# A decoder of six sublayers on one core: an attention's heads put in place by two transfers of 256 KB instead of four of 128 KB

## The chip, the cores and the metric

The kernel runs on one core of a Trainium2 chip. The metric is the device time of one execution in microseconds (us); the median of three runs before the change is 1601.11 us (1593.27 to 1602.95).

## What is computed

Sixteen sequences of 256 tokens and 256 channels go through two decoder layers of three sublayers each. After every sublayer its output is added to the stream and the sum is normalised (`_layernorm`):

```python
x = _layernorm(x + _L0_attn_ref(x, ...))            # 16 heads of 16, rotary, self
x = _layernorm(x + _L0_xattn_ref(x, ctx, ctx, ...)) # 8 heads, gated mLSTM-like mix
x = _layernorm(x + _L0_ffn_ref(x, ...))             # quantised, ternary weights
x = _layernorm(x + _L1_attn_ref(x, ...))            # 16 heads of 16, self
x = _layernorm(x + _L1_xattn_ref(x, ctx, ctx, ...)) # 16 heads of 16, cross
x = _layernorm(x + _L1_ffn_ref(x, ...))             # relu, 1024 wide
```

Three of the six are softmax attentions with 16 heads of 16 channels, and the change concerns these three only:

```python
attn = softmax(einsum('bhqd,bhkd->bhqk', q, k) * scale)
out = einsum('bhqk,bhkd->bhqd', attn, v)
return out.transpose(0, 2, 1, 3).reshape(B, N, C) @ w_proj + b_proj
```

## The kernel before

The 16 sequences are dealt to four lanes (L = 0 to 3), four sequences each, one after the other in a lane. Each lane has its own buffers and runs the same list of steps (`lane_steps`); the lanes are interleaved so that an engine that would wait for one lane works for another. Which lane an engine serves next is not decided while it runs: `TURNS` holds one string of digits per engine, and `engine_program` deals each lane's steps out in that order. So each of the five instruction queues (TensorE, ScalarE, VectorE, GpSimd, SyncE) is a fixed list worked off in order, with semaphore waits in it. `PLACES` says which PSUM banks a step of TensorE uses, and `FILL` how many extra products of a constant (line 688, tile `cst`, results never read) it does at the head of a step; both are fixed tables too.

One attention of one lane runs so. `max` (line 785 on TensorE, line 1198 on VectorE) finds the largest score of each row, `negmax` lays the negated maxima beside the queries (a small transfer, line 672), `exp` (line 804, then ScalarE's Exp on line 1025) makes the weights of two heads at a time in eight units, `pv` multiplies them with the values. The weights of a unit go to one of three places in turn: two halves of `PB` and, for units 2 and 5, the tile `YX`. The value products (line 822) come in four steps, `pv` 0 to 3, for four heads each. Each value has beside it a column of ones, so that a product of 32 rows holds the 16 channels of a head and 16 copies of the sum of its weights, row by row in turn. Two steps share a PSUM bank: ScalarE copies the results of `pv` 0 and 1 into `U[:, 0:2]`, and those of 2 and 3 into `U[:, 2:4]` (line 1029; each copy raises `u_ready`). The first of the two steps raises `pv_half`.

In `U` channels and sums alternate from row to row. The step `spread` on SyncE (line 668) sorts them with transfers inside SBUF: the channels to `OT`, the sums to `sums`, which are the two halves of `YX`, 64 rows per transfer, all four transfers behind one wait for the second copy. Then ScalarE's step `heads` waits for all of them (`spread`), takes the logarithm of the sums (line 1032) and the exponential of the negated logarithm (line 1034), GpSimd multiplies the channels with it (line 1357), and TensorE's step `proj` (line 712, `psum<-W_o,YX`) multiplies with the output weights. VectorE adds the stream (line 1204) and normalises. There are 3 × 16 = 48 such attentions. `W_o`'s rows are laid out to match the places of the heads when the weights are loaded.

SyncE's queue also carries everything else that moves: the queries and keys through DRAM (lines 653 and 656 out, line 662 back, `QK<-heads_dram`), the inputs (593, 597) and the outputs (675).

Of the kernel before, what the change touches and what calls it, by code (L numbers as in the profile page):

```python
# [16 lines left out]
P = 128  # L17
# [40 lines left out]
def lane_steps():  # L58

    out = []  # L60

    def add(name, occ=0, unit=0, ahead=0):
        out.append((name, occ, unit, ahead))

    def attention(a):
        if a:
            add("xT", a + 1)
            add("xb", a + 1)
            for name in ("qk", "stack"):
                for j in range(2 if a == 1 else 1):  # L70
                    add(name, a, j)
        if a == 1:
            add("v", 1)
        for u in range(PAIRS):
            add("max", a, u)
        add("negmax", a)
        for u in range(PAIRS):
            add("exp", a, u)
            if u in (2, 4, 6):
                add("pv", a, (u - 2) // 2)  # L80
        add("pv", a, 3)
        add("spread", a)
        add("heads", a)
        if a == 1:
            add("qk", 2, 1)
            add("stack", 2, 1)
            add("v", 2)
        if a == 2:
            add("loadx", 0, 0, 1)
        add("proj", a)  # L90
        add("norm", NORM_OF[a])

    attention(0)
    add("xT", 1)
    add("xb", 1)
    add("gates")
    add("vm")
    add("turn")
    add("decay", 0, 0)
    add("decay", 0, 1)  # L100
    add("mix", 0, 0)
    add("decay", 0, 2)
    add("mix", 0, 1)
    add("mixv", 0, 0)
    add("decay", 0, 3)
    add("mix", 0, 2)
    add("mix", 0, 3)
    add("mixv", 0, 1)
    add("mixnorm")
    add("mixvar")  # L110
    add("mixscale")
    add("mixout")
    add("norm", 1)
    add("quant")
    for t in range(TT):
        add("gate", 0, t)
        add("up", 0, t)
    for t in range(TT):
        add("hT", 0, t)
    add("down")  # L120
    add("norm", 2)
    attention(1)
    attention(2)
    add("loadc", 0, 0, 1)
    add("xT", 4)
    add("xb", 4)
    for u in range(4):
        add("up1", 0, u)
    add("xT", 0, 0, 1)
    for t in range(TT):  # L130
        add("rope", 0, t, 1)
    add("ctx", 0, 0, 1)
    add("v", 0, 0, 1)
    add("down1", 0, 0)
    for name in ("qk", "stack"):
        for j in range(2):
            add(name, 0, j, 1)
    add("down1", 0, 1)
    add("norm", 5)
    add("store")  # L140
    add("xb", 0, 0, 1)
    return out


def lane_program(lane):
# [7 lines left out]
    for at in range(-1, batches):  # L153
# [56 lines left out]
        "3312203100002112121112232223300003331311102313222303030011112223300220010331121012312203033300111102"  # L210
        "2323123002112333200112103302031133222233"),
    "sp": (
        "4330022110000111414022212303331224330000101114400122220001233331011122320122300331120000013322311111"
        "0232322230123333213233000011110122220001001323330111232200122303210000013332123111110232222323013333"
        "2133230000011110122220000123313301121032201202320000013333121212130111332222012333333123230000111101"
        "020202210013333012113022231223333210323213"),
}

PLACES = (
# [106 lines left out]
def decoder_kernel(nc, x, ctx, consts, w_qkv0, w_proj0, w_gates, b_gates, w_gate, w_up, w_down,  # L326
# [3 lines left out]
    with es:  # L330
# [50 lines left out]
        OT = XT_  # L381
        sums = [v[:, 0].rearrange("p (k t) -> p k t", k=KT) for v in YX]

        VA, ones = ([v[:, :].rearrange("p (n d c) -> p n d c", d=HD, c=2)[:, :, :, n] for v in V] for n in range(2))
        VM = [v[:, 0:TT * MH * MHD].rearrange("p (t h c) -> p t h c", t=TT, c=MHD) for v in V]
        R = [v.rearrange("p u t -> p (u t)").bitcast(F32) for v in KS]
        parts = [v[:, :, :].rearrange("p g t -> p (g t)").bitcast(F16).rearrange("p (a j k t) -> p a j k t", a=2, j=2, k=KT)
# [196 lines left out]
        def _(sp):  # L584
            def by_pair(w, k, u):
                return w.rearrange("(e k u d) n -> k u e d n", e=2, k=KT, d=HD)[k, u]
# [25 lines left out]
            def weights(unit):  # L612

                if unit < LANES:
                    sp.wait_ge(stacked[unit], 32)
                if unit == 1:
                    sp.wait_ge(permuted, 4)
                if unit == 0:
                    load(mask_loaded, (W_g[:, :, :], kt_major(w_gates[0:4 * P, :])), (g_late, kt_major(w_gates[4 * P:6 * P, :])),
                         (b_g[:, :], b_gates.rearrange("(n a) -> n a", a=1)), (c_future, consts[:, C_FUT:C_ALL]),  # L620
                         *[(c_sel[n], consts[:, C_SEL + 512 * n:C_SEL + 512 * n + 512]) for n in range(2)])
                elif unit < 4:
                    a = unit - 1
                    w = (w_proj0, w_proj1, wo)[a]
                    load(weights_loaded[a], *[(W_o[32 * u:32 * u + 32, a, k], by_pair(w, k, u)) for k in range(KT) for u in range(4)])
                    if a == 1:
                        load(weights_loaded[a], (W_qkv[1][:, :, 2 * DIM:], kt_major(w_qkv1)[:, :, 2 * DIM:]))
                    elif a == 2:
                        load(weights_loaded[a], (W_x[:, 2], kt_major(wv)))
                        load(bias_loaded, (col_b[:, 2 * KT:], cols[2 * DIM:].rearrange("(k p) -> p k", p=P)),  # L630
                             *[(col_b[:, n:n + 1], by_row(n)) for n in range(2 * KT)])
                else:
                    sp.wait_ge(ternary, len(TERNARY))
                    load(weights_loaded[3], (W_1[:, :, :], kt_major(w1)), (W_2[:, :, :], kt_major(w2)))

            for it, name, L, occ, unit in engine_program("sp"):
                row = (it * LANES + L) * TOK
                if name == "first":
                    first()
                elif name == "weights":  # L640
                    with nc.allow_non_contiguous_dma(reason="columns of biases, once"):
                        weights(unit)
                elif name == "loadc" and it:
                    sp.wait_ge(x_ready[L], (it * NORMS - 1) * TT)
                    load_c(L, it)
                elif name == "loadx" and it:
                    sp.wait_ge(turned[L], nth(TURNED, it - 1, "quant"))
                    load_x(L, it)
                elif name == "qk":
                    j = unit  # L650
                    sp.wait_ge(hi_ready[L], it * HI_STEPS + QK_AT[occ, unit])
                    for slot in ((0, 2) if j else (0, 1)):
                        sp.dma_start(heads_dram[L][j, :, slot].rearrange("k r u t -> (r u) k t"), parts[L][:, 0, j])\
                          .then_inc(part_out[j][L], 16)
                    sp.wait_ge(lo_ready[L], it * HI_STEPS + QK_AT[occ, unit])
                    sp.dma_start(heads_dram[L][j, :, 1 if j else 2].rearrange("k r u t -> (r u) k t"), parts[L][:, 1, j])\
                      .then_inc(part_out[j][L], 16)
                elif name == "stack":
                    if (it, occ) == (0, 0):
                        sp.wait_ge(slots_set, 16 * LANES)  # L660
                    sp.wait_ge(part_out[unit][L], (it * ATTN + occ + 1) * 48)
                    sp.dma_start((KS if unit else QS)[L][:, :, :], heads_dram[L][unit].rearrange("k s r u t -> (k s r) u t"))\
                      .then_inc(stacked[L], 16)
                elif name == "spread":
                    sp.wait_ge(u_ready[L], it * U_USES + U_AT[occ] + 2)
                    for home, other in ((OT, 0), (sums, 1)):
                        for g in range(2):
                            sp.dma_start(home[L][64 * g:64 * g + 64, :, :], U[L][other:P:2, g:4:2, :])\
                              .then_inc(spread[L], 16)
                elif name == "negmax":  # L670
                    sp.wait_ge(nmT_ready[L], it * ATTN + occ + 1)
                    sp.dma_start(QS[L][48:113:64, :, :], nmT[L]).then_inc(nm_row[L], 16)
                elif name == "store":
                    sp.wait_ge(x_ready[L], (it * NORMS + NORMS) * TT)
                    sp.dma_start(out[bass.ds(row, TOK), :].rearrange("(t p) d -> p t d", p=P), stream(L, it))\
                      .then_inc(stored[L], 16)
# [279 lines left out]
        def _(act):  # L956
# [18 lines left out]
            for step in engine_program("act"):  # L975
# [22 lines left out]
                elif name == "qk":  # L998
# [3 lines left out]
                    else:  # L1002
                        if it == 0:
                            act.wait_ge(bias_loaded, 80)
                        if unit:
                            act.wait_ge(spread[L], (it * ATTN + 2) * 64)
                        for k in range(KT):
                            act.activation(parts[L][:, 0, unit, k], b[:, k * TOK:(k + 1) * TOK], ACT.Identity,
                                           bias=col_b[:, KT * unit + k:KT * unit + k + 1]).then_inc(hi_ready[L], 1)
# [18 lines left out]
                    b = wait_full(act, it, name, L, occ, unit - 1)  # L1028
                    act.activation(flat2(U[L][:, unit - 1:unit + 1, :]), b[:, 0:512], ACT.Copy).then_inc(u_ready[L], 1)  # L1029
                elif name == "heads":  # L1030
                    act.wait_ge(spread[L], (it * ATTN + occ + 1) * 64)
                    log = own(act.activation(flat2(sums[L][:, :, :]), flat2(sums[L][:, :, :]), ACT.Ln))
                    wait_own(log)
                    act.activation(flat2(sums[L][:, :, :]), flat2(sums[L][:, :, :]), ACT.Exp, scale=-1.0)\  # L1034
# [381 lines left out]
```

## Time and profile before

| | us |
|---|---|
| median of three runs | 1601.11 |
| the profiled execution, its own time | 1596.03 |
| its span, first to last instruction | 1594.0 |
| TensorE busy (matmul) | 1478.0 |
| VectorE busy | 1146.6 |
| ScalarE busy | 985.3 |
| GpSimd busy | 289.3 |

All numbers of the profile are of one execution on the one core, with a mean granted TensorE clock of 0.986 of full speed. In a group of instructions the busy time of all of them comes first, then the mean of one, then the idle time of the engine just before them and whose work ended it. SyncE's transfers are listed as `SPq`: the duration there is what the issue takes in the queue, and "to landing" runs from the issue's start until the data has arrived. The extra products of line 688 count as busy time of TensorE.

### The profile page before, as it was taken

What the parts mean: (1) busy time and instruction counts of PE and PEld (TensorE: products, weight loads), DVE (VectorE), ACT (ScalarE), POOL (GpSimd) and SP (SyncE); (2) the same over time, 40 slices, a digit from 0 to 9 for tenths busy, and PEclk for the clock granted to TensorE, in tenths of its full rate; (3) what the DMA queues carried; (4) which work ended last, traced back from release to release, by engine and by line L of the source; (5) the groups of instructions that cost most, each with busy time, mean ns of one, the idle gap of its engine ahead of it and who ended that gap; (6) DMA issues with size and microseconds to landing.
All of it is one profiled execution on the core that took longest, in us unless ns stands there. A gap on an engine that the chain in (4) does not pass through costs nothing. (4 is left out here: it accounts for less than half of the span.)

```text
span 1594.0 us, 31275 instructions
## 1 busy us (share of the span) xinstructions
PE 1478.0 (93%) x12244; PEld 961.6 (60%) x12266; DVE 1146.6 (72%) x2007; ACT 985.3 (62%) x1749; POOL 289.3 (18%) x277
## 2 busy tenths in 40 slices
PE   6889999999998998999999998999999999999998
PEld 3555656566675664656766565555676656565657
DVE  3987989856468797865656789876655789986642
ACT  1477666765657755585465865765645686666662
POOL 5121110122221110102222111102122221011010
PEclk8999999999999998999999999999999999999999
DMA  7420243433322112343341121334333202143310
GB/s 252 144 74 28 61 123 111 137 95 108 102 72 61 46 62 59 118 123 106 88 119 54 28 60 30 101 114 116 111 96 93 68 15 67 41 131 109 107 38 30
DMA packets 142721, 139.49 MB, mean 88 GB/s; under 512 B 12914, under 2 KB 128370, under 8 KB 142578
## 3 DMA queue, kind: packets, MB, share of 16 engines
q1 hardware_dynamic: 139714, 131.34, 28.8%
q10 hardware_dynamic: 2864, 6.16, 1.2%
q8 instruction: 100, 1.64, 0.4%
q14 instruction: 43, 0.35, 0.1%
HBM read 68.91 MB, written 42.99 MB: 70 GB/s over the span
## 5 line engine op out<-in xcount | busy, mean ns | idle before, releaser
L1198 DVE TENSOR_REDUCE nm<-psum 128x4 f16<-128x1024 f32 x384 | 453.7, 1223 | 114.4 <-PE psum L785 113.3
L1025 ACT ACTIVATE PB<-psum 128x1024 f32<-128x1024 f32 x288 | 287.5, 1023 | 96.6 <-PE psum L804 94.7
L822 PE MATMUL psum<-PB,V 128*32 128x256 f32 x2304 | 204.7, 385 | 8.8 <-ACT PB L1025 5.1
L1357 POOL TENSOR_TENSOR YX<-YX 128x512 f32<-128x512 f32 x48 | 60.9, 1269 | 598.1 <-ACT YX L1034 598.0
L785 PE MATMUL psum<-QK 48*128 48x256 f16 x1536 | 134.3, 274 | 30.7 <-DMA QK<-heads_dram 10.3
L804 PE MATMUL psum<-QK 49*128 49x256 f16 x1536 | 138.1, 274 | 8.7 <-DVE nm L1198 3.7
L1363 POOL TENSOR_TENSOR XO<-XO,row_b 128x512 f32<-128x512 f32 x80 | 102.5, 1287 | 171.8 <-ACT YX L997 171.8
L688 PE MATMUL psum<-cst 128*128 128x256 f32 x360 | 115.8, 426 | 9.0 <-DMA cst<-in_consts 3.2
L785 PEld LDWEIGHTS psum<-QK 48*128 48x128 f16 x1536 | 57.3, 94 | 102.3 <-issue 52.1
L943 PE MATMUL psum<-YX,W 128*128 128x256 f32 x512 | 118.9, 385 | 0.1
L951 PE MATMUL psum<-W,PB 128*128 128x256 f32 x512 | 117.8, 384 | 0.0
L822 PEld LDWEIGHTS psum<-PB,V 128*32 128x32 f32 x2304 | 77.9, 109 | 65.3 <-issue 18.4
L804 PEld LDWEIGHTS psum<-QK 49*128 49x128 f16 x1536 | 53.8, 94 | 102.5 <-issue 60.0
L1025 ACT ACTIVATE YX<-psum 128x1024 f32<-128x1024 f32 x96 | 98.0, 1023 | 20.4 <-PE psum L804 20.1
L1138 DVE TENSOR_SCALAR XO<-YX,mv,rstd 128x256 f32<-128x256 f32 x192 | 80.5, 462 | 36.1 <-ACT rstd L973 36.0
L943 PEld LDWEIGHTS psum<-YX,W 128*128 128x128 f32 x512 | 94.7, 190 | 18.5 <-issue 4.8
L951 PEld LDWEIGHTS psum<-W,PB 128*128 128x128 f32 x512 | 96.9, 192 | 14.0 <-issue 0.8
L822 PE MATMUL psum<-YX,V 128*32 128x256 f32 x768 | 102.2, 387 | 2.7 <-ACT PB L1025 2.5
L1029 ACT ACTIVATE U<-psum 128x512 f32<-128x512 f32 x112 | 66.8, 597 | 51.3 <-PE psum L822 41.7
L712 PE MATMUL psum<-W_o,YX 128*128 128x256 f32 x384 | 93.8, 387 | 1.3 <-POOL YX L1357 1.0
L997 ACT ACTIVATE YX<-psum 128x512 f32<-128x512 f32 x80 | 47.9, 598 | 59.2 <-PE psum L699 40.9
L688 PEld LDWEIGHTS psum<-cst 128*128 128x128 f32 x360 | 61.6, 198 | 35.0 <-issue 12.0
(172 smaller groups left out, 2702.9 us busy)
## 6 DMA issues: line engine op xcount, KB each, us to landing
QK<-heads_dram SPq DMA_DIRECT2D x96, 512.0 KB, 3.9
heads_dram<-U SPq DMA_DIRECT2D x288, 128.0 KB, 2.0
YX<-U SPq DMA_DIRECT2D x192, 128.0 KB, 3.4
XO<-in_x SPq DMA_DIRECT2D x16, 256.0 KB, 4.2
YX<-in_ctx SPq DMA_DIRECT2D x16, 256.0 KB, 3.6
out<-XO SPq DMA_DIRECT2D x16, 256.0 KB, 2.5
W<-in_w SPq DMA_DIRECT2D x2, 1024.0 KB, 7.0
heads_dram<-PB ACTq DMA_DIRECT2D x4, 256.0 KB, 8.9
```

The source lines that it names most:

```text
L688: pe.matmul(b[:, 0:2 * P], ident, cst[:, 0:2 * P], start=True, stop=True)
L712: ins = pe.matmul(bank[:, t * DIM:(t + 1) * DIM], xt(k)[:, t * P:(t + 1) * P], w[:, k], start=(k == 0), stop=(k == n - 1))
L785: ins = pe.matmul(b[:, e * 512 + t * TOK:e * 512 + (t + 1) * TOK], QS[L][r, unit, t * P:(t + 1) * P], KS[L][r, unit, :], start=True, stop= ...
L804: ins = pe.matmul(b[:, e * 512 + t * TOK:e * 512 + (t + 1) * TOK], KS[L][r, unit, t * P:(t + 1) * P], QS[L][r, unit, :], start=True, stop= ...
L822: ins = pe.matmul(b[SLOT * j:SLOT * j + SLOT, at:at + TOK], value(L, t, e, u), src, start=(t == 0), stop=(t == TT - 1))
L943: ins = pe.matmul(b[:, m * TOK:(m + 1) * TOK], W_1[:, k, c:c + P], XT_[L][:, k, :], start=(k == 0), stop=(k == KT - 1))
L951: ins = pe.matmul(b[:, 0:DIM], hid1(L, k)[:, unit * P:(unit + 1) * P], W_2[:, k], start=(k == 0), stop=(k == IT - 1))
L1025: act.activation(weights_of(L, unit), b[:, 0:1024], ACT.Exp, scale=HD ** -0.5)\
L1029: act.activation(flat2(U[L][:, unit - 1:unit + 1, :]), b[:, 0:512], ACT.Copy).then_inc(u_ready[L], 1)
L1138: dve.tensor_scalar(stream(L, it)[:, t], Y[L][:, t], mv[L][:, t, 0:1], rstd[L][:, t:t + 1], ALU.subtract, ALU.mult).then_inc(x_ready[L], 1)
L1198: dve.tensor_reduce(nm[L][:, :, :, unit].rearrange("p t e -> p e t"), b[:, 0:1024].rearrange("p (e t k) -> p e t k", e=2, t=TT), AX.X, ALU ...
L1363: pool.tensor_tensor(stream(L, it), stream(L, it), row_b[:, occ:occ + 1, :].to_broadcast([P, TT, DIM]), ALU.add).then_inc(xb_ready[L], 1)
```

## The change

The order of the two kinds of columns is exchanged (ones first), which puts the sums on the even rows of `U` and the channels on the odd ones. With that, two neighbouring rows of `U` (2 KB each: two of its four groups) are, one behind the other, one row of `YX` (sums, then channels). So one transfer moves two groups of all 128 rows of `U` into 64 rows of `YX`: 256 KB, and two such transfers do it all. The first needs only the first copy into `U`, and `YX` free of weights, which it is when `pv` 2 is through (`pv_half`); the second waits for the second copy. The counts that `heads` and one step of the next attention wait for go from 64 to 32 for each attention, and the rows of `W_o` are loaded in the order that fits the new places.

```diff
+        add("spread", a, 0)
         add("pv", a, 3)
-        add("spread", a)
+        add("spread", a, 1)
...
-        VA, ones = ([v[:, :].rearrange("p (n d c) -> p n d c", d=HD, c=2)[:, :, :, n] for v in V] for n in range(2))
+        ones, VA = ([v[:, :].rearrange("p (n d c) -> p n d c", d=HD, c=2)[:, :, :, n] for v in V] for n in range(2))
...
-  load(weights_loaded[a], *[(W_o[32 * u:32 * u + 32, a, k], by_pair(w, k, u)) for k in range(KT) for u in range(4)])
+  load(weights_loaded[a], *[(W_o[32 * u:32 * u + 32, a, k], by_pair(w, u // 2, 2 * k + u % 2)) for k in range(KT) for u in range(4)])
...
                 elif name == "spread":
-                    sp.wait_ge(u_ready[L], it * U_USES + U_AT[occ] + 2)
-                    for home, other in ((OT, 0), (sums, 1)):
-                        for g in range(2):
-                            sp.dma_start(home[L][64 * g:64 * g + 64, :, :], U[L][other:P:2, g:4:2, :])\
-                              .then_inc(spread[L], 16)
+                    sp.wait_ge(u_ready[L], it * U_USES + U_AT[occ] + 1 + unit)
+                    if unit == 0:
+                        sp.wait_ge(pv_half[L], nth(HALVES, it, f"pv{occ}2"))
+                    sp.dma_start(YX[L][64 * unit:64 * unit + 64, :, :].rearrange("p a n -> p (a n)"),
+                                 U[L][:, 2 * unit:2 * unit + 2, :].rearrange("q g t -> q (g t)")).then_inc(spread[L], 16)
...
-                            act.wait_ge(spread[L], (it * ATTN + 2) * 64)
+                            act.wait_ge(spread[L], (it * ATTN + 2) * 32)
...
-                    act.wait_ge(spread[L], (it * ATTN + occ + 1) * 64)
+                    act.wait_ge(spread[L], (it * ATTN + occ + 1) * 32)
```

Of the tables only SyncE's string in `TURNS` changes: it has 48 digits more, one for each first half of a `spread`. The lists of the other four engines, `PLACES` and `FILL` are as they were (line numbers behind the first edit are one higher).

The list of SyncE at about 1075 us of the trace, before (lane numbers stand in the semaphores' names; `YX<-U` is the spread):

```order
L662 DMA QK<-heads_dram 128x2048 [waits k_out1]
L653 DMA heads_dram<-U 128x2x256 [waits hi_ready1]
L653 DMA heads_dram<-U 128x2x256
L656 DMA heads_dram<-U 128x2x256 [waits lo_ready1]
L668 DMA YX<-U 64x2x256 [waits u_ready2]
L668 DMA YX<-U 64x2x256 x3
L662 DMA QK<-heads_dram 128x2048 [waits q_out1]
L668 DMA YX<-U 64x2x256 [waits u_ready0]
L668 DMA YX<-U 64x2x256 x3
L672 DMA QK<-GN 2x8x256 [waits nmT_ready3]
```

The same place with the change:

```order
L663 DMA QK<-heads_dram 128x2048 [waits k_out1]
L654 DMA heads_dram<-U 128x2x256 [waits hi_ready1]
L654 DMA heads_dram<-U 128x2x256
L657 DMA heads_dram<-U 128x2x256 [waits lo_ready1]
L669 DMA YX<-U 64x2x512 [waits pv_half2,u_ready2]
L669 DMA YX<-U 64x2x512 [waits u_ready2]
L663 DMA QK<-heads_dram 128x2048 [waits q_out1]
L669 DMA YX<-U 64x2x512 [waits pv_half0,u_ready0]
L669 DMA YX<-U 64x2x512 [waits u_ready0]
L673 DMA QK<-GN 2x8x256 [waits nmT_ready3]
```

Nothing but the spreads differs. The first half stands directly ahead of the second, here and in all 48 places, so no other step lies between the two, and none changes its place among the others.

A second place, at about 482 us, before:

```order
L672 DMA QK<-GN 2x8x256 [waits nmT_ready2]
L668 DMA YX<-U 64x2x256 [waits u_ready1]
L668 DMA YX<-U 64x2x256 x3
L675 DMA out<-XO 128x2x256 [waits x_ready3]
L668 DMA YX<-U 64x2x256 [waits u_ready2]
```

And with the change:

```order
L673 DMA QK<-GN 2x8x256 [waits nmT_ready2]
L669 DMA YX<-U 64x2x512 [waits pv_half1,u_ready1]
L669 DMA YX<-U 64x2x512 [waits u_ready1]
L676 DMA out<-XO 128x2x256 [waits x_ready3]
L669 DMA YX<-U 64x2x512 [waits pv_half2,u_ready2]
```

The output of lane 3 stands behind two issues where it stood behind four.

## Rows read from the trace of the kernel before

**Rows 1.** The page, part 1: busy time, share of the span and instructions.

```profile
PE 1478.0 (93%) x12244; PEld 961.6 (60%) x12266; DVE 1146.6 (72%) x2007; ACT 985.3 (62%) x1749; POOL 289.3 (18%) x277
```

**Rows 2.** A stretch: length, busy of each engine, granted clock, DMA share, GB/s.

```profile
100.00:1560.00 1460.00, 1371.91 (x11590) 890.28 (x11613) 1065.12 (x1897) 941.68 (x1678) 256.27 (x236) 0.99 0.29 82
```

**Rows 3.** Line 668, all 192 issues: duration ns, who waited, landing us (min/median/max).

```profile
L668 SPq DMA_DIRECT2D YX<-U x192: 593/608/1782, 82.9 to 1554.7; - x192
...
  ACT YX L1032: 22.1, 18
...
DMA to landing us min/median/max: 2.8/3.4/4.7
```

**Rows 4.** Timeline of the last attention, all engines: start us, us, what, idle before.

```profile
1547.05 0.41 PE L822 MATMUL psum<-YX,V 128*32 128x256 f32 x2
...
1550.72 1.07 PE L822 MATMUL psum<-PB,V 128*32 128x256 f32 x16
...
1551.86 0.60 ACT L1029 ACTIVATE U<-psum 128x512 f32<-128x512 f32 x1 [0.43 <-PE psum L822]
...
1552.48 2.85 SPq L668 DMA_DIRECT2D YX<-U  x4
...
1557.94 0.63 ACT L1032 ACTIVATE YX<-YX 128x512 f32<-128x512 f32 x1
...
1559.31 1.27 POOL L1357 TENSOR_TENSOR YX<-YX 128x512 f32<-128x512 f32 x1 [6.53 <-ACT YX L1034]
1562.19 1.89 PE L712 MATMUL psum<-W_o,YX 128*128 128x256 f32 x8
```

**Rows 5.** Line 712 (all its products): idle time of TensorE, by releaser.

```profile
  POOL YX L1357: 1.5, 3
```

**Rows 6.** The 18 waits of line 1032, each with 6 us behind: columns as in 2.

```profile
488.32:494.68 6.36, 5.34 (x72) 3.69 (x64) 4.02 (x6) 3.32 (x7) 1.27 (x1) 1.00 0.01 2
...
sum 126.94, PE 123.11 PEld 91.42 DVE 87.72 ACT 69.99 POOL 35.59; mean PE 7.24 PEld 5.38 DVE 5.16 ACT 4.12 POOL 2.09
```

**Rows 7.** Timeline of SyncE, then ScalarE, 1074 to 1091 us.

```profile
1075.40 2.64 SPq L668 DMA_DIRECT2D YX<-U  x4
...
1079.14 2.58 SPq L668 DMA_DIRECT2D YX<-U  x4
...
1085.85 0.63 ACT L1032 ACTIVATE YX<-YX 128x512 f32<-128x512 f32 x1 [2.01 <-DMA YX<-U]
```

**Rows 8.** The page, part 6: issues, KB each, median us from issue to landing.

```profile
QK<-heads_dram SPq DMA_DIRECT2D x96, 512.0 KB, 3.9
...
XO<-in_x SPq DMA_DIRECT2D x16, 256.0 KB, 4.2
```

**Rows 9.** Line 662, all 96 issues: duration ns, who waited, landing us.

```profile
L662 SPq DMA_DIRECT2D QK<-heads_dram x96: 319/333/597, 38.8 to 1510.8; - x96
...
  PE psum L785: 10.3, 14
```

**Rows 10.** The extra products: the page's part 5, then TensorE's timeline 1469 to 1473.

```profile
L688 PE MATMUL psum<-cst 128*128 128x256 f32 x360 | 115.8, 426 | 9.0 <-DMA cst<-in_consts 3.2
...
1471.33 0.70 PE L688 MATMUL psum<-cst 128*128 128x256 f32 x2
1471.86 1.46 PE L712 MATMUL psum<-W_o,YX 128*128 128x256 f32 x6
```

**Rows 11.** Timeline of SyncE and of TensorE, 625 to 640 us.

```profile
629.64 3.59 SPq L662 DMA_DIRECT2D QK<-heads_dram  x2
...
633.41 2.69 SPq L668 DMA_DIRECT2D YX<-U  x4
...
636.85 0.40 PE L785 MATMUL psum<-QK 48*128 48x256 f16 x4 [1.04 <-DMA QK<-heads_dram]
```

**Rows 12.** The page, part 2: packets of all transfers.

```profile
DMA packets 142721, 139.49 MB, mean 88 GB/s; under 512 B 12914, under 2 KB 128370, under 8 KB 142578
```

More of the change, by code:

```diff
@@ L212 @@
     "sp": (
[L213 to L216, printed above, removed]
+        "4330022110000111414022212300333112224333000010111440001222200011233331011122232001223300331112000001"
+        "3322231111102332322230012333321132233300001111012222000011001323330111223220001223303211000001333221"
+        "2311111023322223230013333211332233000001111001222200001123313301122100322012023320000011333312212121"
+        "301113332222001233333311232233000011110100202022110013333012113002222331223333211032233213"),
 }
```

## The prediction

> **What bounds the kernel now.** I read the shares first: TensorE is busy for 1478.0 of 1594.0 us, 93%, VectorE 72%, ScalarE 62% [rows 1]. The stretch between start and end shows the same: from 100 to 1560 us TensorE is idle for 88.1 of 1460 us, at a granted clock of 0.99 [rows 2]. So what is worth time is what TensorE waits for, and its order of work is fixed. The next view was therefore who waits for the step that changes, first on ScalarE, then on TensorE.
>
> The four transfers of an attention are a visible delay. In the last attention the second copy into `U` ends at 1552.46, the four issues fill SyncE from 1552.48 for 2.85 us, and the logarithm starts at 1557.94, 5.5 us behind the copy [rows 4]. One issue takes 608 ns and one transfer lands 3.4 us after its issue began [rows 3]: three issues and a landing are 1.8 + 3.4 = 5.2 us, the same within 0.3. ScalarE stands still for these transfers 18 times in 48, for 22.1 us in all [rows 3]. But TensorE is two steps further: it waits for GpSimd's multiplication ahead of the output product 3 times, for 1.5 us in all [rows 5]. In the last attention the multiplication is through at 1560.58 and the product starts at 1562.19, since TensorE had other work [rows 4].
>
> **The change, part by part.**
>
> *Issues.* 192 issues of 0.608 us, 117 us of SyncE, become 96. The new access patterns are plain rows, like those of the stacked queries, whose issue takes 0.333 us [rows 9]; with 0.333 and 0.608 as bounds I take 0.45, about 43 us. SyncE is otherwise mostly waiting, so this counts only where something stands behind.
>
> *The landing that `heads` waits for.* Now it is one transfer of 256 KB issued behind the second copy. No row has such a transfer inside SBUF. Below, 128 KB land in 2.8 us at best [rows 3]; above, 256 KB from DRAM in 4.2 and 512 KB in 3.9 [rows 8]. I take 3.4, the median of today's transfers, which have company from their three neighbours as this one has from less. So the logarithm could start 3.4 us behind the copy instead of 5.2 to 5.5: 2 us earlier (0.9 to 2.7), in each of 48 attentions, 96 us of waiting inside the lanes. The SBUF — State Buffer page of the Trainium skill (section "Door 1: The DMA port swizzle") says that a transfer whose partitions are one half of the 128 reaches 8 of 16 ports, at some 218 GB/s; with its fixed 2 us that makes an estimate of 3.2 us for 256 KB, and a sum that differs from mine by nothing that counts.
>
> *The first half.* It leaves when `pv` 2 is through and the first copy is done. In the last attention `pv` 2 is at 1547.05, `pv` 3 at 1550.72 and the copy ends at 1552.46 [rows 4], so it has over 4 us and has landed by then. Where TensorE has no other work between, the lead is `pv` 3 and the copy, 1.07 + 0.60 = 1.7 us, and the two halves overlap a little.
>
> *The added wait.* SyncE now waits for `pv_half` and the first copy. Both are always earlier than the second copy, for which it waited at the same place, and nothing stands between the halves. So no step is held longer than before, and what stands behind a spread leaves about 2 us sooner when it was ready. This costs nothing.
>
> *What TensorE gets of it.* The 1.5 us of direct waits go. For the rest, ScalarE's 22.1 us must reach TensorE. I took each of the 18 waits with the 6 us behind it: TensorE is busy in 123.11 of 126.94 us of these [rows 6]. Of the 3.8 us idle, 1.0 lies in the one window shown beside the sum (6.36 less 5.34), which is a direct wait for GpSimd and counted above. So 0 to 2.8 us more; I take half, 1.4. In other words ScalarE loses 22 us at these places but has slack behind them. Even of a product that gets its input sooner the extra products stay: 115.8 us of them are in the list, such as the two just ahead of an output product at 1471.33 [rows 10].
>
> *What the queue gets.* Where a spread delays the queue, as at 1075.40, where four issues are followed by four more for another lane from 1079.14, whose `heads` waits 2.01 us [rows 7], the next steps come sooner. What TensorE waits for there are the stacked queries and keys, 10.3 us in 14 waits [rows 9]. But such a load stands ahead of the spread in the example shown [rows 11], and I found no wait of TensorE that a spread ahead of the load made. I take 0, at most 2.
>
> *The rest.* The exchanged columns are written with the same stride, by the same instructions, and the output weights are loaded by as many transfers as before: 0, since neither count nor shape changes.
>
> Sum: 1.5 + 1.4 + 0 = 2.9 us, 3 rounded. Against the profiled execution's 1596.03 that gives 1593. Its time lies 5.1 below the median of the runs, so for a median of runs I say 1601.1 − 3 = **1598 us**.
>
> **The rivals.**
>
> *A. The 2 us reach the end.* If what ScalarE wins goes to TensorE in full, because a lane that is ahead stays ahead, the time falls by 1.5 + 22.1 = 23.6 us, to 1577.5; half of it gives 1589. For it: TensorE does idle 88 us in the middle [rows 2], and the slack may be spent later than in the 6 us that I looked at. Against it: 97% busy where the gain arises [rows 6], and fixed orders on every engine, made with the old delays.
>
> *B. The early half gets in the way (slower).* The first half leaves right behind a load of queries or keys for which TensorE waits, as at 633.41, directly behind the loads issued from 629.64, with TensorE waiting 1.04 us at 636.85 [rows 11]. Today the four transfers come there later and in small pieces. If a load in flight lands later by 1.3 us, the distance of a crowded landing from a median one (4.7 − 3.4, [rows 3]), and all 14 waits [rows 9] grow by that, it costs 18 us, to 1619; with a third of them it is 6, less my 3, and 1604. It decides over the gain from three such waits on. Against it: a DMA share of 0.29 [rows 2], and the same bytes move as before.
>
> *C. Merging gives little.* If 256 KB land only after 4.2 us or more, `heads` starts 1 us earlier instead of 2, some of the 18 waits stay, and the time is 1600 to 1601. The trace shows transfers held by the issue rate: four issues of 0.6 us against one landing of 3.4. The Perfetto Trace Analysis page of the Trainium skill (section "DMA Optimizations") says that with mostly idle DMA engines splitting a transfer may let the whole finish sooner. That speaks for the four; by it the merged landing is late, as in this case, and the sum would be 0 to 1 us in place of 3.
>
> **How the numbers follow.** My forecast (1594 to 1601) gets 0.68, A 0.14, B 0.08, C 0.10. Runs of this kernel lie within 0.6% of each other, so 1% is about what can be told from no change. Faster by over 1% means under 1585.1: two thirds of A, 0.10. Slower by over 1% means above 1617.1: only B at nearly its full price, 0.03. Within: 0.87. The range: half of A below, B's usual size above and 5 us of difference between executions, 1585 to 1606.
>
> **What would show it.** The wait of the logarithm for the spread falls from 22.1 to under 5 us and starts 3 to 4 us behind the copy (A, B and the forecast agree; C says 4.2 or more, and 8 us or more left). TensorE's wait for GpSimd's multiplication falls from 1.5 to near 0. TensorE's busy time stays at 1478 and its idle time falls by about 3 us; in A by 15 or more. The waits for stacked queries and keys stay at 10 us; in B they rise to 15 or more. The count of packets falls by some 13,800: 24,576 of 1 KB give way to 12,288 of 2 KB, and 16 small ones of each of 96 transfers go, from 142,721 to about 128,900 [rows 12]; if it stays, the pieces are not what I think. I am wrong if TensorE's idle time moves by over 10 us either way, or if the granted clock, which no term of mine touches, changes.

## The result: slower by 0.6%

The changed kernel takes 1603.99 us (median of 20 runs, 1597.65 to 1613.97) against 1595.64 (median of 20, 1590.65 to 1602.95); the ratio is 1.0058, 95% interval 1.0045 to 1.0070. I had forecast 1598 and 3 us of gain. The time lies in my range, but it moved the other way, by some 9 us: less than the 1% that I had called the limit of what can be told, and with 20 runs clear of no change. My 1598 was 3 us below a median of three runs, 1601.11; 3 us below the 1595.64 of the twenty it would have been 1593. So 1604 lies nearer to the forecast than the change in time does, by the luck of a high start.

### The profile page after: what moved, and what is told of

It reads as the page before. It is cut to its first block and busy times, and to the rows that moved or that the text cites. A ratio compares the mean times of both kernels' runs of the same rounds, so it can differ in the third digit from the quotient of the medians.

```text
span 1603.6 us, 31249 instructions
## 1 busy us (share of the span) xinstructions
PE 1480.2 (92%) x12266; PEld 960.6 (60%) x12266; DVE 1147.6 (72%) x2007; ACT 985.2 (61%) x1749; POOL 289.4 (18%) x277
## 5 line engine op out<-in xcount | busy, mean ns | idle before, releaser
L786 PE MATMUL psum<-QK 48*128 48x256 f16 x1536 | 134.5, 274 | 36.7 <-DMA QK<-heads_dram 16.5
```

The source lines that it names most:

```text
L786: ins = pe.matmul(b[:, e * 512 + t * TOK:e * 512 + (t + 1) * TOK], QS[L][r, unit, t * P:(t + 1) * P], KS[L][r, unit, :], start=True, stop= ...
```

## The profile after, and where the time went

The page of the changed kernel, part 1 (busy time) and the packet count, which answer to [rows 1, 12]:

```profile
span 1603.6 us, 31249 instructions
...
PE 1480.2 (92%) x12266; PEld 960.6 (60%) x12266; DVE 1147.6 (72%) x2007; ACT 985.2 (61%) x1749; POOL 289.4 (18%) x277
...
DMA packets 128896, 139.48 MB, mean 87 GB/s; under 512 B 11378, under 2 KB 102258, under 8 KB 128754
```

No engine does more work (TensorE's 2 us come with 22 matmul records that the trace of before lacks). TensorE's idle time went from 116.0 to 123.4 us, the span from 1594.0 to 1603.6. The packets fell as worked out, to 128,896.

Now the transfers: line 669 (the spread), line 663 (the loads of queries and keys) and the output product's wait, as in [rows 3, 9, 5]; below a line its duration in ns, who waited (us, times), and the landing in us.

```profile
L669 SPq DMA_DIRECT2D YX<-U x96: 532/546/1545, 80.8 to 1562.0; - x96
...
  ACT YX L1033: 13.6, 11
...
DMA to landing us min/median/max: 3.9/4.3/7.3
...
L663 SPq DMA_DIRECT2D QK<-heads_dram x96: 320/333/551, 39.3 to 1520.3; - x96
...
  PE psum L786: 16.5, 15
...
DMA to landing us min/median/max: 3.1/3.9/6.6
...
  POOL YX L1358: 1.6, 4
```

There are three things to see. A spread of 256 KB lands in 3.9 us at best, 4.3 as a rule and 7.3 at worst, where I had taken 3.4. ScalarE's waits for it fell only from 22.1 to 13.6 us, and TensorE's wait for the multiplication did not fall at all (1.5 to 1.6). And TensorE waits 16.5 us for the loads of queries and keys, where it waited 10.3: 6.2 us of the 9.6 that the span grew. Of the 14 waits before, 4 (4.6 us in all) had a spread issued between 7 and 1 us ahead of their end; of the 15 with the change it is 11 (13.3 us). So the growth lies where a spread is beside the load. About 1.9 of the rest is a longer wait at the very start, 13.8 against 11.9 us for the first transposed input; the other traces below have 12.1 to 14.1 there, and not in the order of their times, so that belongs to the single execution.

Other transfers are later too. Here are the lines of part 6 with the change; before, the medians were 4.2, 3.6 and 2.5 us:

```profile
XO<-in_x SPq DMA_DIRECT2D x16, 256.0 KB, 4.9
YX<-in_ctx SPq DMA_DIRECT2D x16, 256.0 KB, 4.5
out<-XO SPq DMA_DIRECT2D x16, 256.0 KB, 3.1
```

And SyncE's DMA queue moves the same bytes in fewer packets but takes more time for them. The line of part 3 (packets, MB, the time of the packets as a share of 16 engines' span), before and with the change:

```profile
q1 hardware_dynamic: 139714, 131.34, 28.8%
...
q1 hardware_dynamic: 125890, 131.33, 30.3%
```

One place shows the mechanism in small. The timeline before, SyncE and TensorE, 325 to 335 us (start, duration, what, idle before):

```profile
328.55 0.33 SPq L662 DMA_DIRECT2D QK<-heads_dram  x1
330.26 2.65 SPq L668 DMA_DIRECT2D YX<-U  x4
...
330.48 1.99 PE L705 MATMUL psum<-CT,W_x 128*128 128x256 f32 x8
332.40 0.39 PE L785 MATMUL psum<-QK 48*128 48x256 f16 x4
```

The same place with the change:

```profile
334.93 0.33 SPq L663 DMA_DIRECT2D QK<-heads_dram  x1
335.36 1.23 SPq L669 DMA_DIRECT2D YX<-U  x2
...
336.27 1.99 PE L706 MATMUL psum<-CT,W_x 128*128 128x256 f32 x8
336.64 0.60 SPq L594 DMA_DIRECT2D XO<-in_x  x1
...
339.93 0.39 PE L786 MATMUL psum<-QK 48*128 48x256 f16 x4 [1.66 <-DMA QK<-heads_dram]
```

The load is issued, and the first half of the spread 0.43 us behind it, where the first of four came 1.71 us behind. Before, the load landed in 3.1 us, and TensorE did not wait at 332.40; now it lands in 4.9, and TensorE stands for 1.66 us. The halves are not alone here: the next input (line 594, 256 KB from DRAM) leaves 1.71 us behind the load, where before it left 4.4 us behind. The place of [rows 11] has no such input. There the spread stood directly behind the load before as well (0.5 us, four transfers), and the load landed in 3.8 us; with two halves 0.44 us behind it lands in 5.5, and the wait grew from 1.04 to 1.60:

```profile
646.37 0.39 PE L786 MATMUL psum<-QK 48*128 48x256 f16 x4 [1.60 <-DMA QK<-heads_dram]
```

And where two spreads and a load follow each other [rows 7], the second logarithm waits 2.60 us, where it waited 2.01; the spread was issued from 1086.64 and all of it had landed 8.1 us later:

```profile
1086.64 1.39 SPq L669 DMA_DIRECT2D YX<-U  x2
...
1094.79 0.63 ACT L1033 ACTIVATE YX<-YX 128x512 f32<-128x512 f32 x1 [2.60 <-DMA YX<-U]
```

## The experiments

Two theories. **1:** what costs is that the first half leaves early and so gets in the way of loads that TensorE waits for. **2:** what costs is the target: 256 KB into 64 rows that form one half of the 128 move slowly, whenever they leave. Ratios are against the kernel before on the same chip, from 12 runs of each version and 17 to 35 of the kernel before, with 95% intervals; the traces' waits are of one execution each, and a single execution can lie some us beside its kernel's median.

### Each shape alone

```diff
+            for _ in range(4):
+                sp.dma_start(all_of(YX[1][0:64, :, :]), all_of(U[0][:, 0:2, :])).then_inc(stored[0], 16)
+                sp.wait_ge(stored[0], next(alone))
+            ...   # five more shapes in the same way, behind the last store
```

> The kernel before, with 24 transfers behind its last store, one at a time: four each of 256 KB from 128 rows into the 64 rows of one half (the change's), 128 KB from 64 into 64 rows (the kernel's before, in 1 KB pieces), 256 KB from 128 rows into every other row, 256 KB from 128 into 128 rows, 256 KB from 64 into 64 rows of one half, 128 KB from 64 into 64 rows in 2 KB pieces. Theory 1 (the early leaving is what costs): the shape matters little, all 256 KB shapes land within 0.3 us of each other near 3.3. Theory 2 (the target rows are what costs): the ones into 64 rows of one half take about 4.0, the ones into every other row or 128 rows 3.2 to 3.4, and the 128 KB one 2.9. The time of the whole is before plus some 80 us of these transfers.

Issue and landing, in the order of the expectation's list:

```profile
L685 SPq DMA_DIRECT2D YX<-U x4: 532/541/555, 1594.0 to 1606.0; - x4
DMA to landing us min/median/max: 3.9/4.0/4.0
...
L688 SPq DMA_DIRECT2D YX<-U x4: 593/599/605, 1609.9 to 1618.3; - x4
DMA to landing us min/median/max: 2.8/2.8/2.8
...
L691 SPq DMA_DIRECT2D YX<-U x4: 532/538/544, 1621.1 to 1628.2; - x4
DMA to landing us min/median/max: 2.3/2.4/2.4
...
L694 SPq DMA_DIRECT2D U<-U x4: 465/474/490, 1630.6 to 1637.5; - x4
DMA to landing us min/median/max: 2.2/2.3/2.3
...
L697 SPq DMA_DIRECT2D U<-U x4: 462/472/492, 1639.8 to 1648.6; - x4
DMA to landing us min/median/max: 2.9/2.9/2.9
```

(The sixth, 128 KB in 2 KB pieces, took 2.6.) The change's shape takes 4.0 us with nothing beside it; the same bytes into every other row take 2.4, less than the 2.8 of half as many bytes in the old shape. Theory 1's "within 0.3 us" is refuted. Theory 2 had the 4.0 and expected 3.2 to 3.4 for the good shapes, which were faster still. But the last line breaks a simple reading of theory 2 too: 256 KB into 64 rows of one half take only 2.9 when they also come from one half.

### Which property of the shape

```diff
+                sp.dma_start(all_of(YX[1][32:96, :, :]), all_of(U[1][:, 0:2, :])).then_inc(stored[1], 16)
+            ...   # and four more shapes, as before
```

> The kernel before, with five more shapes behind its last store, one transfer at a time, four each: 256 KB from 128 rows into rows 32 to 95; 256 KB from rows 0 to 63 into 128 rows; 256 KB from every other row into rows 0 to 63; 128 KB from 128 rows into rows 0 to 63; 256 KB from every other row into 128 rows. If what makes 4.0 us is that the target lies in one half (rows 0 to 63 or 64 to 127), rows 32 to 95 land in 2.4 to 2.9, and every other row into rows 0 to 63 in 3.5 or more. If it is the two counts of rows (128 against 64) together with one half, the last of these lands in 2.9, and rows 0 to 63 into 128 rows near 4.0 as well.

Measured: 128 rows into rows 32 to 95, 2.9 us; rows 0 to 63 into 128 rows, 3.0; every other row into rows 0 to 63, 3.9; 128 KB from 128 rows into rows 0 to 63, 2.7; every other row into 128 rows, 2.4. So the counts of rows are not it: every other row into rows 0 to 63 is 64 rows into 64 and takes 3.9, while a target of 64 rows that reaches into both halves (32 to 95) takes 2.9. What the slow shapes share is a source that lies in both halves and a target in one. The four transfers of the kernel before had this property as well (every other row into one half), with half the bytes each. From 128 to 256 KB such a transfer grows by 1.3 us (2.7 to 4.0).

### A load with a transfer right behind it, and two halves

```diff
+                sp.dma_start(QS[1][:, :, :], queries).then_inc(stored[0], 16)
+                sp.dma_start(all_of(YX[1][0:64, :, :]), all_of(U[1][:, 0:2, :])).then_inc(stored[1], 16)
+            ...   # with other shapes behind the load, and the two halves behind each other
```

> The kernel before, with seven sets of transfers behind its last store, four times each: the load of queries alone (512 KB from DRAM); the same with, right behind it, 256 KB into one half of the rows, 256 KB into every other row, or 128 KB in the old shape; the two halves of the change behind each other; the same into every other row; 256 KB into rows 64 to 127 alone. Theory 2 (slow target rows): the load alone lands in 3.1 us, with the half behind it in 4.5 or more, with every other row in 3.5 or less, with the old one in 3.3 or less; the two halves land 6 us behind the first issue, into every other row under 3.5; rows 64 to 127 as slow as rows 0 to 63, 4.0. Theory 1: the load is delayed by any transfer behind it, in proportion to its bytes, by the same for both 256 KB shapes.

The load alone, with the half behind it, and with every other row behind it (landing of the load):

```profile
L691 SPq DMA_DIRECT2D QK<-heads_dram x4: 320/326/339, 1589.3 to 1599.2; - x4
...
DMA to landing us min/median/max: 3.2/3.3/3.3
...
L694 SPq DMA_DIRECT2D QK<-heads_dram x4: 319/319/320, 1602.4 to 1618.8; - x4
...
DMA to landing us min/median/max: 4.2/4.5/4.7
...
L698 SPq DMA_DIRECT2D QK<-heads_dram x4: 319/319/319, 1624.3 to 1638.0; - x4
...
DMA to landing us min/median/max: 3.6/3.8/3.9
```

With one 128 KB transfer of the old shape behind it the load lands in 3.7. So every transfer behind a load delays it somewhat (0.4 us by 128 KB, 0.5 by 256 KB into every other row, both more than theory 2 had said), and the change's half delays it by 1.2. The same bytes in two shapes give 0.5 and 1.2, which refutes theory 1's "by the same for both". The transfer behind the load lands later too, the half in 5.1 us and every other row in 4.1. Four old transfers or both halves behind a load were not timed. The two halves behind each other land in 4.3 and 5.5 us, the second issued 0.6 us later: all is there 6.1 us behind the first issue. Into every other row it is 3.1. Rows 64 to 127 alone take 4.0, as rows 0 to 63.

### Size and moment, two by two

Both halves behind the second copy:

```diff
-                    sp.wait_ge(u_ready[L], it * U_USES + U_AT[occ] + 1 + unit)
+                    sp.wait_ge(u_ready[L], it * U_USES + U_AT[occ] + 2)
```

> The changed kernel, with both halves issued behind the second copy. Theory 1 (the early half delays loads of queries and keys that TensorE waits for): the waits for these loads fall back from 16.5 to 10 to 12 us, the time to 0.3% above before or less, though the logarithm now starts 6 us behind the copy. Theory 2 (what costs is that 256 KB into one half of the rows move slowly, whenever they leave): the loads are delayed as much or more, ratio 1.005 or more, ScalarE's waits for the spread 25 us or more.

Measured 1.0046 (1.0029 to 1.0062). Most of the loss stays without any early half, against theory 1's 1.003 at most; theory 2's 1.005 lies in the interval. ScalarE's waits for the spread rise to 38.2 us, its landing to 5.5, as theory 2 had it; the loads' waits are 12.1 us, as theory 1 had it. That trace is of the fastest of the 12 executions (1599.56 against a median of 1605.38), so where the loss of the median goes it does not show.

Each half as two transfers of 128 KB, the first two early:

```diff
-                    sp.dma_start(YX[L][64 * unit:64 * unit + 64, :, :].rearrange("p a n -> p (a n)"),
-                                 U[L][:, 2 * unit:2 * unit + 2, :].rearrange("q g t -> q (g t)")).then_inc(spread[L], 16)
+                    for a in (1, 0):
+                        sp.dma_start(YX[L][64 * unit:64 * unit + 64, a, :],
+                                     U[L][a:P:2, 2 * unit:2 * unit + 2, :].rearrange("q g t -> q (g t)")).then_inc(spread[L], 16)
...   # and ScalarE's counts back from 32 to 64
```

> The changed kernel's places and its early first half, but each half as two transfers of 128 KB (channels, sums), four in all. Theory 1: the early leaving is kept, so it stays slow, 1.004 to 1.006, and the waits for queries and keys stay near 16 us. Theory 2: with the old size the old rate comes back, ratio 0.998 to 1.001.

Measured 1.0022 (1.0001 to 1.0042), landing 3.1 us, ScalarE's waits 6.7, the loads' waits 14.8. That is between the two theories.

The same four, all behind the second copy (both edits):

> The changed kernel's places, with four transfers of 128 KB, all behind the second copy as in the kernel before. Theory 2: the time of before, 0.999 to 1.001, and from it to the same with an early first half (1.0022) is what leaving early costs in itself, 0.002 or less. Theory 1: clearly better than with the early half, by 0.003 or more.

Measured 1.0008 (0.9988 to 1.0028): the time of before. The loads' waits are 8.8 us, ScalarE's 15.4.

### The first half held where a load stands ahead of it

```diff
-                    sp.wait_ge(u_ready[L], it * U_USES + U_AT[occ] + 1 + unit)
+                    sp.wait_ge(u_ready[L], it * U_USES + U_AT[occ] + (2 if behind_load else 1 + unit))
```

> The changed kernel, with the first half held until the second copy only at the 20 places of 48 where it stands directly behind a load of queries or keys. Theory 1: the waits for the loads fall to 10 to 12 us and nearly all of the loss goes, ratio 0.998 to 1.002. Theory 2: no better than the change, 1.004 or more. If neither, the loss lies in the start or elsewhere.

(`behind_load` is true where the step just ahead in SyncE's list is such a load.) Measured 1.0029 (1.0008 to 1.0050): about half of the loss goes by the ratio, but its interval overlaps the changed kernel's, and it lies between the two theories' ranges. The loads' waits did not fall to theory 1's 10 to 12 us; they were 20.4, and ScalarE's for the spread 26.2. So this edit alone does not say much. A held half has the other one right behind it, and loads meet both; that this is what raised the waits was not tested.

### The same bytes into every other row

```diff
-  (W_o[32 * u:32 * u + 32, a, k], by_pair(w, u // 2, 2 * k + u % 2))
+  (W_o[64 * (u % 2) + u // 2:64 * (u % 2) + 64:2, a, k], by_pair(w, u // 2, 2 * k + u % 2))
...
-                    sp.dma_start(YX[L][64 * unit:64 * unit + 64, :, :].rearrange("p a n -> p (a n)"),
+                    sp.dma_start(YX[L][unit:P:2, :, :].rearrange("p a n -> p (a n)"),
```

> The changed kernel with its early first half, but each 256 KB go into every other row of YX (the first half into the even rows, the second into the odd ones) in place of one half of the rows; the output weights are laid out to match. Alone such a transfer landed in 2.4 us, the change's in 4.0. Theory 2 (the target rows are what costs): landings near 2.6, the waits for queries and keys at 10 to 12 us, ScalarE's waits near 2 us, and the gain I had forecast: ratio 0.997 to 1.000. Theory 1 (leaving early is what costs): still 1.002 to 1.005.

Measured 0.9993 (0.9977 to 1.0009). The early half, the size and all counts are the change's; only the target rows (and with them the layout of the output weights) differ, and the loss is gone. The DMA queue's time is down to 26.1% of 16 engines' span, with the same packets and bytes. The trace, lines 669 and then TensorE's wait for the loads:

```profile
L669 SPq DMA_DIRECT2D YX<-U x96: 532/546/817, 81.0 to 1553.3; - x96
...
  ACT YX L1033: 1.8, 2
...
DMA to landing us min/median/max: 2.3/2.4/4.9
...
PE psum L786 <- DMA QK<-heads_dram: 9.3, 12, 1.6
```

The same with both halves behind the second copy:

> The same with both halves behind the second copy. Theory 2: two transfers at this rate land some 3.2 us behind the copy, still 2 us sooner than before, and the ratio is 0.997 to 1.000, the same as with the early half within 0.002. Theory 1: better than with the early half, by 0.002 or more.

Measured 0.9981 (0.9967 to 0.9996), median 1595.39 against 1597.95. The same version (`e6` in the next expectation) was run again:

> The kernel of e6 once more, unchanged. If its 0.9981 is real, the ratio is 0.996 to 0.9995 again; if it was chance, 1.000 or more is as likely.

Measured 0.9987 (0.9970 to 1.0005), median 1596.17 against 1597.64. This is the version that comes out of the study. It is faster than the changed kernel, since the intervals lie apart; over the kernel before it gains 0.1 to 0.2%, clear of no change in one of two measurements.

### Without the first transfer

```diff
-                elif name == "spread":
+                elif name == "spread" and unit == 0:
+                    pass
+                elif name == "spread":
...   # and ScalarE's counts from 32 to 16
```

> The changed kernel without its first transfer (the heads of its half are left out of the result, the products are done on what lies there); the second one is as in the change, 256 KB into one half of the rows. Theory 2: half of the slow traffic gone, none of it beside another half: ratio 0.998 to 1.001, waits for queries and keys 10 to 12 us. Theory 1: the same, since nothing leaves early. It is the bound for what the first half costs: the change's 1.0058 less this.

Measured 0.9999 (0.9979 to 1.0019), which both theories allow; the loads' waits are 14.1 us, above the 10 to 12 expected. The first half with all that it meets costs the whole 0.6%. But the loads' waits are still well above the 10.3 of before while the time is not, so the sum of these waits in one trace is no measure of the loss.

The same in the other shape:

> Every other row, and without the first transfer (its heads are left out of the result as well). It has the fewest and fastest transfers of all: whatever an earlier start of the logarithm and an emptier DMA can give shows here. My forecast's 3 us: ratio 0.997 to 0.999. If what ScalarE wins reached the end in full: 0.985.

Measured 0.9977 (0.9960 to 0.9994), 3.7 us: the bound for what a sooner spread can bring here, as half of its bytes are gone besides. ScalarE's waits are down to 1.1 us. In this shape the first half costs 0.0016 (0.9993 less 0.9977), in the change's 0.0059.

## Why the prediction was wrong

**The step that failed is the landing** ("I take 3.4", and "a sum that differs from mine by nothing that counts"). Alone it is 4.0, and two of them, where the second is issued 0.6 us behind the first, need 6.1 us, longer than the 5.2 to 5.5 of four old transfers. Between 2.8 and 4.2 I had chosen by the median of today's transfers. They too go from rows in both halves into one half, but with half the bytes: alone they take 2.8 us, and in this shape the second 128 KB add 1.3. No row showed that growth. By rival C, a late landing alone would have left 0 to 1 us of gain; that the time rose instead comes by the next two points, the first half and the queue.

I also took the half-of-the-ports figure of the Trainium skill's SBUF — State Buffer page (section "Door 1: The DMA port swizzle") as agreeing with me and went on. The traces say that it is not the target's half alone (2.9 us from one half into one half) but a source over both halves with it.

**The first half was not free** ("the two halves overlap a little", for which the sum had no term). In 13 of the 48 places the second half is issued within 0.6 to 0.7 us of the first and lands in 5.4 to 6.4 us. ScalarE's waits lie there: 9 of its 11, 12.5 of 13.6 us, stand behind halves issued at most 1.2 us apart. Of the sum, the 1.5 us of direct waits for GpSimd did not go (1.6 were left).

**What the queue gets, taken as 0, was a loss: rival B.** I had its mechanism, a half leaving right behind a load, its example and its price of 6 to 18 us, and gave it 0.08. That its lower case, 1604, is the measured median is luck: it was counted from 1601. The loads' waits rose from 10.3 to 16.5 us, as its mark of 15 or more said. What I held against it, a DMA share of 0.29 and equal bytes, was the error: over the mean of a span the DMA is mostly idle, but the load in flight and the half meet in the same 4 us, and equal bytes are not equal time. The measured delay of a load is 1.2 us by one half against 0.4 by one old transfer; I had estimated 1.3. What rival B had not was the shape: with halves into every other row, just as early, the waits are 9.3 us. And how the loss of the median reaches TensorE is argued from single traces, not shown: the version with both halves late loses 0.46% with 12.1 us of these waits in its trace, the one with the first half held 0.29% with 20.4, and the one without the first half nothing with 14.1.

**How much is the shape, how much the moment.** From one half to every other row the ratio falls by 0.0065 with the early half (1.0058 to 0.9993) and by 0.0065 without (1.0046 to 0.9981). From late to early it rises by 0.0012 in the one shape, 0.0012 in the other, 0.0014 with four transfers. So the shape is the cause, nearly all of it. The repeated late version makes the second of these 0.0006. The differences for the moment have one sign, but each is within the intervals of its pair, so a cost of leaving early in itself is possible and not shown.

**What held.** The gain of a sooner start was rightly small: I had 2.9 us, and by their ratios the kernels in which the spread does land sooner gain 1.1 us (every other row, early), 3.0 and 2.1 (late, two measurements) and 3.7 at the bound, with ScalarE's waits nearly gone. Rival A, with 12 to 24 us, is refuted by the same runs: some 20 us less of waiting on ScalarE reach the end as 1 to 4. The count of packets came out as worked out; the issue takes 0.55 us where I took 0.45; no run tells what that costs. Rival C had the right direction for the landing and missed that slow transfers also hold up others.

**Open.** Why a source over both halves and a target in one are slow together, while a source over both halves with a target over both takes 2.3 to 2.9, and a source in one half with a target in the same one 2.9, no run tells. Of the 9.6 us between the two traces 6.2 are the loads' waits and up to 1.9 the start; where the rest lies was not followed up. Why the loads' waits rose to 20.4 us with the held half is not settled.

## What to carry to other kernels

Before merging transfers inside SBUF, look at which rows they leave and reach, and time the merged shape alone with four copies behind the kernel's end: one run would have told that the merged transfer takes 4.0 us, not 3.4, and that another choice of rows takes 2.4. If the rows of a target can be chosen (here by the order of a weight's rows), interleave the pieces over all rows and don't stack them in halves. And a transfer made early is made beside something: look at what is in flight just ahead of it in the queue and who waits for that, not at the mean share of the DMA.

## What the runs showed of the hardware that I had not expected

- 256 KB inside SBUF, alone, from issue to landing (medians of four): 128 rows to 128 rows 2.3 us, to every other row 2.4, every other row to 128 rows 2.4; from one half to the same half 2.9, to rows 32 to 95 2.9, one half to 128 rows 3.0; every other row to one half 3.9, 128 rows to one half 4.0. Only the last two have a source in both halves and a target in one.
- A transfer of 128 KB from rows in both halves into one half is slower (2.6 to 2.8 us) than one of 256 KB into every other row or all rows (2.3 to 2.4).
- A load of 512 KB from DRAM, 3.3 us alone, lands in 3.7 with 128 KB of the old shape issued right behind it, in 3.8 with 256 KB into every other row and in 4.5 with 256 KB from 128 rows into one half.
- The SBUF — State Buffer page of the Trainium skill (section "Door 1: The DMA port swizzle") gives transfers to rows 0 to 63 half the ports and so half the rate of those to all rows. The traces agree in direction (2.9 against 2.3 us where both sides have the same rows), but the largest difference, 4.0 against 2.9 with the same target, is not in it; there the measurement decides.
